# Taps of a convolution by ScalarE, their sums by GpSimd, gate and scan by VectorE

## What is computed

```python
def reference(x, ...):
    x = x + 0.5 * ffn(layernorm(x))          # 32 experts of 64, top 4, and a shared one of 128
    x = x + mixer(layernorm(x))
    x = x + 0.5 * ffn(layernorm(x))

def mixer(x, ...):                           # D = 128 features
    gate, val = split(x @ W_in.T)
    g = sigmoid(gate)
    v = conv1d(val, conv_w, depthwise, 5 taps, padding 2) + conv_b
    h[t] = tanh(a_param) * h[t-1] + g[t] * v[t]     # along each sequence
    res = x + h @ W_out.T
    return layernorm(res) * ln_w + ln_b
```

## Time and profile before

| | us |
|---|---|
| median of 3 runs | 672.98 (671.9 to 673.3) |
| the profiled execution | 672.07, its span 670.3 |
| TensorE busy | 656.8 |
| VectorE busy | 548.9 |
| GpSimd busy | 446.5 |
| ScalarE busy | 420.7 |

### The profile page before, as it was taken

The page is one execution under the profiler, slowest core; times in us unless marked ns, Lnnn a source line. Parts: engine busy times, 40 slices in busy tenths (PEclk is TensorE's granted clock), DMA queues, the critical chain, the costliest instruction groups (busy, mean ns, idle before and its releaser), DMA issues. The chain is left out here.

```text
span 670.3 us, 10334 instructions
## 1 busy us (share of the span) xinstructions
PE 656.8 (98%) x3083; PEld 530.8 (79%) x3083; DVE 548.9 (82%) x1540; ACT 420.7 (63%) x804; POOL 446.5 (67%) x452
## 2 busy tenths in 40 slices
PE   8899999999999999999999999999999999999997
PEld 7787888888888887888888888888878778777675
DVE  5888889979878877879879898788979868867765
ACT  4756666675676656766476755767676566655554
POOL 2346667866776766766677775867676776776564
PEclk9999999999999999999999999999999999999999
DMA  9664909248091925629084470917419074380561
GB/s 223 144 142 99 188 11 226 51 110 162 26 224 42 215 53 124 133 80 206 17 187 101 108 147 22 227 41 168 104 32 223 2 172 100 75 181 17 118 137 32
DMA packets 60232, 78.30 MB, mean 117 GB/s; under 512 B 8176, under 2 KB 27664, under 8 KB 60176
## 3 DMA queue, kind: packets, MB, share of 16 engines
q1 hardware_dynamic: 59600, 77.63, 52.2%
q10 hardware_dynamic: 576, 0.02, 0.1%
HBM read 74.49 MB, written 3.15 MB: 116 GB/s over the span
## 5 line engine op out<-in xcount | busy, mean ns | idle before, releaser
L576 POOL TENSOR_TENSOR hid_lo<-hid,hid_hi 128x512 fp32r<-128x512 f32 x270 | 348.3, 1294 | 188.3 <-ACT hid_hi L689 188.0
L840 DVE TENSOR_TENSOR weighted<-gate_ps,raw 128x512 f32<-128x512 f32 x256 | 175.2, 684 | 69.7 <-ACT gate_ps L681 64.1
L681 ACT ACTIVATE gate_ps<-gate_ps 128x512 f32<-128x512 f32 x256 | 148.7, 581 | 119.7 <-PE gate_ps L1119 116.4
L689 ACT ACTIVATE hid_hi<-hid 128x512 fp32r<-128x512 f32 x272 | 170.4, 626 | 64.4 <-DVE hid L853 61.1
L853 DVE TENSOR_TENSOR hid<-weighted,up_ps 128x512 f32<-128x512 f32 x256 | 174.3, 681 | 8.0 <-issue 0.5
L1190 PE MATMUL down_ps<-hid_lo,wt_hi 128*128 128x512 f32 x272 | 108.0, 397 | 0.2 <-DVE hid_lo L861 0.2
L1187 PE MATMUL down_ps<-hid_hi,wt_hi 128*128 128x512 f32 x272 | 107.8, 396 | 0.0
L1188 PE MATMUL down_ps<-hid_hi,wt_lo 128*128 128x512 f32 x272 | 107.7, 396 | 0.0
L1117 PE MATMUL gate_ps<-xT_hi,wt_hi 128*128 128x512 f32 x170 | 72.0, 423 | 0.0
L1117 PE MATMUL up_ps<-xT_hi,wt_hi 128*128 128x512 f32 x170 | 68.4, 402 | 2.4 <-DVE hid L853 2.3
L1118 PE MATMUL gate_ps<-xT_lo,wt_hi 128*128 128x512 f32 x170 | 67.3, 396 | 0.0
(11 more groups left out here) (187 smaller groups left out, 1108.4 us busy)
## 6 DMA issues: line engine op xcount, KB each, us to landing
raw<-wT_hbm SPq DMA_DIRECT2D x96, 512.0 KB, 11.6
raw<-wT_hbm SPq DMA_DIRECT2D x62, 256.0 KB, 4.5
x_ln<-in_L_attn_x SPq DMA_DIRECT2D x8, 256.0 KB, 4.0
x_res<-in_L_attn_x SPq DMA_DIRECT2D x8, 256.0 KB, 3.7
out_x<-x SPq DMA_DIRECT2D x7, 256.0 KB, 2.3
raw<-in_L_ffn_gate_w SPq DMA_DIRECT2D x4, 256.0 KB, 4.9
raw<-in_L_ffn_up_w SPq DMA_DIRECT2D x4, 256.0 KB, 4.9
raw<-in_L_ffn_down_w SPq DMA_DIRECT2D x4, 256.0 KB, 5.2
```

The costliest lines, as they stand in the source:

```text
L576: nc.gpsimd.tensor_tensor(hid_lo[s][:, :], hid[s][:, :], hid_hi[s][:, :].bitcast(F32), ALU.subtract)\
L681: nc.scalar.activation(bank[:, :] if j else silu_sb[:, :], bank[:, :], ACT.Silu).then_inc(silu_done, 1)
L689: nc.scalar.activation(hid_hi[s][:, :], hid[s][:, :], ACT.Copy).then_inc(hid_hi_done, 1)
L840: V.tensor_tensor(weighted[j % 2][:, :], gate_ps[n % BANKS][:, :], wb[:, j - 1, :], ALU.mult)\
```

## The change

The four tap operations of VectorE become, for each, a product by ScalarE (`tap`, a Copy with the tap as per-partition scale, into one of two new SBUF buffers `tap_of`) and an addition by GpSimd (`add tap`, into a new SBUF buffer `value`, which takes the place of the PSUM bank `mixed` for the convolution). The semaphore `mix` had counted VectorE's six operations; now `tap_done` and `tap_added` count products and sums, `gated` and `mix` the gate and the scan. A product waits until the sum before the last, which read its buffer, is done. The gate waits for all four sums. `add ln_b` moves from tile 16 to tile 9, 8 or 5 of a later unit (and from 12 to 5 in unit 13). In unit 13, transpose, gate product, value product and what follows for the last block go two tiles earlier (value product from tile 11 to 9); in unit 11 the value product goes from 15 to 14.

```diff
-        conv = mixed[:, :].rearrange("p (s t) -> p s t", s=SB)
+        value = sb("value", [P, BLK])
+        conv = value[:, :].rearrange("p (s t) -> p s t", s=SB)
+        tap_of = [sb(f"tap_of{n}", [P, BLK]) for n in range(2)]
...
         PROJECT = {"stats 2": 1.5, "meanvar 2": 2, "norm 2": 2, "normalise 2": 3, "transpose 2": 9, "xT high 2": 9,
                    "xT low 2": 9.5, "mixer gate": 10, "tanh gate": 10, "mixer value": 12, "copy value": 12,
-                   "add ln_b": 16}
+                   "tap": (13, 14, 15, None), "add tap": (15, 16, None, None)}
...
-        MIXER = {"conv": (0, 0, 0, 0, 0.5, 1.5), "y high": 5, "y low": 5, "mixer out": 9, "mixer sum": 12.5,
+        MIXER = {"tap": (None, None, None, 1), "add tap": (None, None, 0, 2), "gate value": 3, "recur": 3.5,
+                 "add ln_b": 9, "y high": 5, "y low": 5, "mixer out": 9, "mixer sum": 12.5,
                  "stats 3": 13}
...
                 # BEGIN, unit 1, block 0
-                ({"conv": (15, 15.5, 16.5, 16.5, None, None)}, 0),
+                  "tap": (14, 14, 15, 16), "add tap": (15, 15, 16, None)}, 0),
...
                 # unit 2, block 0, then block 1
-                ({"conv": (None, None, None, None, 0, 0), "y high": 0, "y low": 1, "mixer out": 6, "mixer sum": 6.5,
+                ({"add tap": (None, None, None, 0), "gate value": 0.5, "recur": 1, "y high": 2, "y low": 2, "add ln_b": 5,
+                  "mixer out": 6, "mixer sum": 6.5,
...
-                  "add ln_b": 16}, 1),
+                  "tap": (14, 15, 15, 16), "add tap": (15, 16, 16, None)}, 1),
...
                 # unit 3, block 1
-                ({"conv": (0, 0, 0, 0.5, 1.5, 2.5), "y high": 3, "y low": 3, "mixer out": 6, "mixer sum": 8,
-                  "stats 3": 12}, 1),
+                ({"add tap": (None, None, None, 0), "gate value": 1, "recur": 1.5, "y high": 3, "y low": 3, "add ln_b": 8,
+                  "mixer out": 6, "mixer sum": 8, "stats 3": 12}, 1),
...
                 # END, unit 11, block 5, then block 6
-                ({"conv": (0.5, 1, 1.5, 2.5, 3.5, 4.5), "y high": 5, "y low": 4, "mixer out": 7, "mixer sum": 7.5,
+                ({"tap": (None, None, None, 1), "add tap": (None, None, 0, 2), "gate value": 3, "recur": 3.5,
+                  "y high": 5, "y low": 5, "add ln_b": 8, "mixer out": 7, "mixer sum": 7.5,
                   "stats 3": 8.5}, 5),
...
-                  "xT low 2": 10.5, "mixer gate": 11, "tanh gate": 13, "mixer value": 15, "copy value": 15,
-                  "add ln_b": 16}, 6),
+                  "xT low 2": 10.5, "mixer gate": 11, "tanh gate": 13, "mixer value": 14, "copy value": 14,
+                  "tap": (15, None, None, None), "add tap": (16, None, None, None)}, 6),
...
                 # unit 12, block 6
-                ({"conv": (0, 0, 0.5, 0.5, 2.5, 3.5), "y high": 5, "y low": 5, "mixer out": 7, "mixer sum": 8,
-                  "stats 3": 8.5}, 6),
+                ({"tap": (None, 0, 1, 1), "add tap": (None, 1, 2, 3), "gate value": 3.5, "recur": 4,
+                  "y high": 5, "y low": 5, "add ln_b": 8, "mixer out": 7, "mixer sum": 8, "stats 3": 8.5}, 6),
...
                 # unit 13, block 7
-                ({"stats 2": 0.5, "meanvar 2": 2, "norm 2": 0, "normalise 2": 2, "transpose 2": 9, "xT high 2": 9,
-                  "xT low 2": 8.5, "mixer gate": 10, "tanh gate": 10, "mixer value": 11, "copy value": 12,
-                  "add ln_b": 12}, 7),
-                ({"conv": (13, 13.5, 14, 14.5, 15, 15.5), "y high": 16, "y low": 16}, 7),
+                ({"stats 2": 0.5, "meanvar 2": 2, "norm 2": 0, "normalise 2": 2, "add ln_b": 5, "transpose 2": 7,
+                  "xT high 2": 7, "xT low 2": 7.5, "mixer gate": 8, "tanh gate": 8, "mixer value": 9, "copy value": 10,
+                  "tap": (11, 11, 12, 13), "add tap": (12, 12, 13, 14), "gate value": 15, "recur": 15.5,
+                  "y high": 16, "y low": 16}, 7),
...
+            def add_tap(b, part):
+                if part == 0:
+                    pool.wait_ge(first_tap_done, b + 1)
+                else:
+                    pool.wait_ge(tap_added, b * TAPS + part)
+                pool.wait_ge(tap_done, b * TAPS + part + 1)
+                nc.gpsimd.tensor_tensor(value[:, :], value[:, :], tap_of[part % 2][:, :], ALU.add)\
+                  .then_inc(tap_added, 1)
...
+            def tap(b, part):
+                act.wait_ge(mix_val_done, b + 1)
+                if b * TAPS + part >= 2:
+                    act.wait_ge(tap_added, b * TAPS + part - 1)
+                nc.scalar.activation(tap_of[part % 2][:, :].rearrange("p (s t) -> p s t", s=SB),
+                                     val_pad[:, :, part + 1:part + 1 + SEQ], ACT.Copy,
+                                     scale=taps_half[:, part + 1:part + 2]).then_inc(tap_done, 1)
...
-            def conv_tap(i, st, t):
...
+            def gate_value(i):
+                dve.wait_ge(tap_added, i * TAPS + TAPS)
                 dve.wait_ge(mix_gate_done, i + 1)
+                V.scalar_tensor_tensor(value[:, :], gate_t[:, :], 1.0, value[:, :], ALU.add, ALU.mult)\
+                 .then_inc(gated, 1)
+
+            def recur(i):
+                dve.wait_ge(gated, i + 1)
                 if i > 0:
                     dve.wait_ge(y_lo_done, i)
+                V.tensor_tensor_scan(y[:, :], decay[:, :], value[:, :], 0.0, ALU.mult, ALU.add).then_inc(mix, 1)
```

More of the change, by code:

```diff
@@ L299, in macaron_kernel @@
         first_tap_done = sem("first_tap_done")
+        tap_done = sem("tap_done")
+        tap_added = sem("tap_added")
+        gated = sem("gated")
         halved_done = sem("halved_done")
@@ L351, in macaron_kernel @@
                   "xT low 2": 10, "mixer gate": 11, "tanh gate": 11, "mixer value": 13, "copy value": 13,
-                  "add ln_b": 16}, 0),
-                ({"conv": (15, 15.5, 16.5, 16.5, None, None)}, 0),
+                  "tap": (14, 14, 15, 16), "add tap": (15, 15, 16, None)}, 0),
                 ({"transpose 1": 0, "xT high 1": 0, "xT low 1": 0, "router 1": 1, "silu logits 1": 3,
@@ L443, in macaron_kernel @@
         LOGITS_READ = 2
-        MIX = K + 1
+        TAPS = K - 1
         block = ctx.enter_context(nc.Block())
@@ L628, in unit @@
                         nc.gpsimd.tensor_tensor(x1_b[:, :, :], x1[b % 2][:, :, :], bc, ALU.add).then_inc(x1_b_done, 1)
+                    for part, b in parts_due(steps, "add tap", j):
+                        add_tap(b, part)
                     for b in due(steps, "y low", j):
@@ L767, in unit @@
                         if b > 0:
-                            act.wait_ge(mix, b * MIX)
+                            act.wait_ge(gated, b)
                         nc.scalar.activation(gate_t[:, :], side[:, :], ACT.Tanh, scale=0.5)\
@@ L777, in unit @@
                         if b > 0:
-                            act.wait_ge(mix, b * MIX)
+                            act.wait_ge(mix, b)
                         nc.scalar.activation(conv, val_pad[:, :, 0:SEQ], ACT.Identity,
@@ L781, in unit @@
                           .then_inc(first_tap_done, 1)
+                    for part, b in parts_due(steps, "tap", j):
+                        tap(b, part)
                     for b in due(steps, "y high", j):
-                        act.wait_ge(mix, b * MIX + MIX)
+                        act.wait_ge(mix, b + 1)
                         nc.scalar.activation(y_hi[:, :], y[:, :], ACT.Copy).then_inc(y_hi_done, 1)
@@ L970, in route_step @@
                     assert st.n == ROUTE
-            def conv_tap(i, st, t):
-                src = val_pad[:, :, t:t + SEQ]
-                if t == 1:
-                    dve.wait_ge(first_tap_done, i + 1)
-                else:
-                    st.wait()
-                st.done(V.scalar_tensor_tensor(conv, src, taps_half[:, t:t + 1], conv, ALU.mult, ALU.add))
-            def gate_value(i, st):
-                dve.wait_ge(mix_gate_done, i + 1)
-                st.wait()
-                st.done(V.scalar_tensor_tensor(conv, gate_t[:, :].rearrange("p (s t) -> p s t", s=SB), 1.0, conv,
-                                               ALU.add, ALU.mult))
-            def recur(i, st):
-                st.wait()
+            def gate_value(i):
+                dve.wait_ge(tap_added, i * TAPS + TAPS)
+                dve.wait_ge(mix_gate_done, i + 1)
+                V.scalar_tensor_tensor(value[:, :], gate_t[:, :], 1.0, value[:, :], ALU.add, ALU.mult)\
+                 .then_inc(gated, 1)
+            def recur(i):
+                dve.wait_ge(gated, i + 1)
                 if i > 0:
                     dve.wait_ge(y_lo_done, i)
-                st.done(V.tensor_tensor_scan(y[:, :], decay[:, :], mixed[:, :], 0.0, ALU.mult, ALU.add))
-                assert st.n == MIX
+                V.tensor_tensor_scan(y[:, :], decay[:, :], value[:, :], 0.0, ALU.mult, ALU.add).then_inc(mix, 1)
             def chain_at(sem, b, length, part):
@@ L1032, in beside @@
```

(12 more changed lines are left out.)

## The result

The changed kernel takes 717.45 us, the median of six runs (714.12 to 719.81). The kernel before, on the same chips, takes 672.44 (671.49 to 673.47). The ratio is 1.0667, interval 1.0635 to 1.0699: 6.7% slower. The forecast was 706.6 with a range of 688 to 716, so the direction and most of the size were right, and the time lies 1.5 us above the range.

What follows compares the result with a forecast made beforehand. The prediction took TensorE's own rate to bound units 1 to 13, so new waits add in full. 672.1 plus 34.5 (12.0 + 2.8 + 5.1 + 6.5 + 4.3 + 3.8) gave 706.6 us, range 688 to 716.

Steps and rivals of the forecast that it cites:

- The bound: Units 1 to 13, 60.9 to 581.6 us: TensorE's own rate bounds, 0.7 us of waits; relieving VectorE buys nothing.
- any new wait that reaches TensorE's queue is added in full: Between 60.9 and 581.6 us, each new TensorE wait lengthens the kernel by its whole duration.
- the sum of 34.5: All added time over the kernel: 12.0 + 2.8 + 5.1 + 6.5 + 4.3 + 3.8 us.
- The wait that decides: Tile 15 of units 4, 6, 8, 10: tap 2 waits for sum 0, transposes 3.0 us late each, 12.0.
- Gate and scan at 3 and 3.5: Middle units: gate and scan, now with two SBUF inputs, are held behind GpSimd; 4 x 0.7 = 2.8 us.
- VectorE 20 us less: Whole kernel, a sign the forecast is right: VectorE's busy time falls by about 20 us.
- Unit 11: Counted like units 5, 7 and 9: late transposes 3.0 us plus gate and scan 0.7 us.
- one layout serves all four seams: After units 4, 6, 8 and 10: the layout worked out in unit 4 holds for all, 3.0 us each.
- The single places: Units 1 to 2, 2 to 3, 12 and 13: ScalarE and gate waits, 5.1, 6.5, 4.3, 3.8; 1.5 us either way each.
- Costs nothing: Moved add ln_b, unit 13's value product at tile 9, the later weight copy: no time added.
- No hold between gate or scan and GpSimd: Rival: VectorE's gate and scan are not held, less 2.8 and 4 x 1.1 us, 699.4 us; chance 0.20.
- Both gate and scan are held in full everywhere: Rival: 1.7 us more at four places and 1.1 at four, 717.8 us; chance 0.10.

Runs made afterwards that it cites:

- the fitted version without holds: Changed kernel with four product buffers, gate_t and the gate's result in PSUM, and tables refitted in units 2, 3, 11, 12 and 13: 676.57 us, ratio 1.0074.
- The seven copies: Kernel before with seven idle 128x512 copies in ScalarE's queue at tile 15 of units 4, 6, 8 and 10: 689.5 us, ratio 1.0253.
- the four copies: Kernel before with four idle 128x512 copies in ScalarE's queue at tile 15 of units 4, 6, 8 and 10: 676.57 us, ratio 1.0064.
- the filler: Kernel before with seven idle ScalarE copies, plus 30 TensorE transposes of 128x128 ahead of the waiting ones in units 5, 7, 9 and 11: 685.71 us.
- the two versions with an operand in PSUM: Changed kernel, two product buffers kept: gate_t in PSUM bank mixed, 709.08 us; the gate's result there too, so the scan reads PSUM, 706.0 us.
- four buffers: Changed kernel with four product buffers instead of two, so a tap waits only for the block before; tables unchanged: 702.34 us, ratio 1.0438.
- the version with the moves alone: Kernel before with add ln_b and unit 13's last-block products at the changed kernel's tiles, convolution left with VectorE: 671.07 us, ratio 0.9991.
- The operand and the buffers together: Changed kernel with four product buffers and gate_t in the PSUM bank mixed: 688.98 us, ratio 1.0255.

## Why the prediction was right or wrong

**The bound: half right.** That TensorE's queue bounds the kernel between 60.9 and 581.6 us, and that VectorE's relief buys nothing there, is borne out: the fitted version without holds has middle units of 39.74 us for 39.83, 39.46 and 39.48, and gains nearly all that it gains in unit 14. But the step "any new wait that reaches TensorE's queue is added in full" failed. It is added, and the clock falls behind it. The forecast had no term for that. In the profiled execution it is 8.5 us, in the median about 11.8; without it the sum of 34.5 stood against 33.5. The seven copies, the four copies and the filler show the cause: 4 waits of 2.8 us cost 17.7 us where they sum to 11.1, 4 of 0.8 cost 4.7 for 3.1 with no lower clock, and with TensorE kept busy the 17.7 become 13.9. Without this term the time would lie in the range: 672.44 + 33.2 is 705.6. That this is so near 706.6 is partly luck, as shown below.

The Trainium skill (TensorE: Matmul & The Clock Gate, What's actually happening) says that the array's clock is released by activity and goes back to half rate when the engine idles, and its section on HAM oscillation describes a loop that pays so at each of its waits. The trace agrees in kind and not in every instance: the two windows of units 5 and 9 above, with the same wait of 2.9 us, have 0.96 and 1.00, and units 2 and 12 have 0.96 behind waits of at most 1.74 us. In before, with 0.7 us of waits in 520 and a full clock, nothing shows this price; it has to be asked of the waits that the forecast itself puts in.

**The wait that decides: right in place, size and chain.** Nine holds of ScalarE of 2.1 to 4.0 us, two of them under the forecast's 2.6 (forecast eight or nine of 2.6 to 4); the transposes' wait is 11.8 us in four units (12.0); one of them 2.94 (3.0). The tap's 0.70 us was 0.72. GpSimd's 42 us of sums should read 41 (32 x 1.29) and were 41.2. Behind this is the only thing worth doing first with such a change: reading three queues in program order.

**Gate and scan at 3 and 3.5: right in mechanism, mixed in size.** Taken were 0.7 us a unit in view; in unit 5 TensorE's wait at tile 6, for weighted of tile 4 behind the scan, is 0.65, and only the scan was held there. That the exclusion is the cause was an argument from the earlier trace rows, and the two versions with an operand in PSUM show it. Its weight in the whole was about right once the clock is set aside: four times 0.7 and four times 1.1 are 7.2 us, and taking the exclusion away gave 11.4 (717.45 to 706.0), of which by the mean clocks of all runs (0.9835 and 0.991) some 5 are clock. The hold is also mutual, which the forecast left out. In unit 11 GpSimd's hid_lo, begun during the scan, takes 1.65 for 1.29:

```profile
502.81 1.21 DVE L1014 TENSOR_TENSOR_SCAN y<-decay,value 128x512 f32<-128x512 f32 x1
```
```profile
503.43 1.65 POOL L583 TENSOR_TENSOR hid_lo<-hid,hid_hi 128x512 fp32r<-128x512 f32 x1 [1.89 <-ACT hid_hi L708]
```

The Trainium skill's rule (SBUF — State Buffer, Who interferes with whom) holds here in both directions.

**VectorE 20 us less: wrong, 10.** The taps took 24.1 with them; gate (5.3), scan (2.2) and `gdiff` (10.2 to 13.2 us in 16, held longer, with GpSimd 40 us busier) gave back 10.5. That makes 13.6 us of durations; the busy time, which counts the overlap of successive operations once, fell by 10.1 (548.9 to 538.8).

**Unit 11: wrong.** It was counted as a middle unit, 3.0 + 0.7, and cost 7.8, of which 1.5 is clock. Its table is another: GpSimd has `norm 2` at tile 0, so sum 3 comes later, the gate waits and is then held (1.77 us), and a routing operation behind it is late for TensorE at tile 4:

```profile
500.25 1.29 POOL L583 TENSOR_TENSOR hid_lo<-hid,hid_hi 128x512 fp32r<-128x512 f32 x1
```
```profile
500.32 1.77 DVE L1006 SCALAR_TENSOR_TENSOR value<-gate_t,value 128x512 f32<-128x512 f32 x1 [0.49 <-POOL value L605]
...
504.52 0.27 DVE L931 TENSOR_TENSOR logit<-tiny,side 128x128 f32<-128x128 f32 x1
```
```profile
504.85 0.66 PE L1213 MATMUL side<-ident,ffn_sb 128*128 128x128 f32 x4 [1.52 <-DVE logit L931]
```

`mixer out`, at tile 7 here and at 9 in the middle units, waits another 0.9 us for y_lo. By the windows the unit is 6.3 longer without the clock for 3.7. The step that failed is the claim that one layout serves all four seams. The late gate is also what four buffers uncover (4.2 us there).

**The single places: about right, somewhat too high.** Without their clock, units 2 and 12 cost 3.5 each (5.1, 4.3), unit 3 5.9 (6.5), 13 and 14 together 2.8 (3.8): 15.7 for 19.7, within the 1.5 each that was allowed but for unit 2, 1.6 under. These are 4.0 us too many, unit 11 was 2.6 too few: that they mostly cancel is luck, and no support for the forecast's sum.

**Costs nothing: right** for `add ln_b` and for the value product at tile 9, by the version with the moves alone (671.07).

**The rivals.** "No hold between gate or scan and GpSimd" was priced at 7.2 us less than the forecast; that kernel was built (706.0) and is 11.4 us below after, some 6 without the clock. "Both gate and scan are held in full everywhere", 717.8 at a chance of 0.10, has nearly the measured time and is not what happened: one of the two was held at each place, never both, and in the middle units TensorE's wait behind them is 0.65 us for the 0.7 taken. Its number stands near 717.45 by luck: it adds 11.2 us to the forecast for holds that did not come, and the clock took 11.8. Removing ScalarE's hold by four buffers, for which 683 was expected, gave 15.1 us, less than half: VectorE's wait for sum 3 grew from 5.9 to 11.6 us, the routing operation's from 1.5 to 4.2, and the clock was low in units 2 and 3 (0.93, 0.92). The operand and the buffers together gave 28.5 where the single ones sum to 23.5. The gains of single repairs did not add up here.

What stays open: why a wait of 2.9 us lowers the clock in unit 5 and not in unit 9, why waits of 1 to 1.8 us lower it in units 2 and 12 and not in unit 3, and how much each of the single places owes to which hold. None of these was tried.

## What to carry to other kernels

Before work is shared out among engines with in-order queues, write the program order of each queue beside the hand-overs: with two buffers a producer can be held behind the consumer's other work, and what stands behind the producer pays, here four times 3 us on a TensorE that had next to no waits. Keep one input of a VectorE operation in PSUM where GpSimd is busy beside it: the place of one operand was worth 21 us in the kernel before. And give each wait that is put on a TensorE without waits a second price, for the clock: four of 2.8 us, 11.1 in all, cost 17.7, and four of 0.8, 3.1 in all, cost 4.7 at a full clock. In between it can go either way: waits of 1.8 us, or two of 1 us close together, lowered the clock in some units and not in others, so the price belongs in the range and not only in the sum.

## What was not expected of the hardware

- TensorE's granted clock went to its lower level behind waits of 2.8 to 3 us in most, not all, units, and behind waits of 1.8 us, or two of about 1 us close together, in some. It stayed at full in the four units with a single wait of 0.8 us; with 30 small transposes put ahead of the waiting ones it was 0.999 to 1.0.
- GpSimd is held as well as VectorE: 1.29 us became 1.65 to 1.74 when a VectorE operation on two SBUF inputs was under way at its start.
- A tap product with a pointer scale took 717 ns where `hid_hi`, a copy of the same shape without one, takes 626. The Trainium skill (ScalarE: Activation LUTs, What ACT_TABLE_LOAD costs) puts a per-partition operand at about 93 ns; the trace agrees, 91.
